# Small matmuls without use behind the groups of the token tail and of the first three expert steps

## What is computed

```python
logits = (X @ gate_w.T).astype(jnp.float32)
scores = jax.nn.sigmoid(logits)
_, idx = jax.lax.top_k(scores + bias[None, :], K)          # K = 4 of E = 32 experts
...
pos = jnp.take_along_axis(jnp.cumsum(onehot, axis=0) - 1, eid[:, None], axis=1)[:, 0]
valid = pos < C
xe = jnp.zeros((E, C, D), x.dtype).at[eid, posc].add(...)
h = jax.nn.silu(jnp.einsum('ecd,edi->eci', xe, W1)) * jnp.einsum('ecd,edi->eci', xe, W3)
ye = jnp.einsum('eci,eid->ecd', h, W2)
...
out = out + jax.nn.silu(X @ sw1.T) * (X @ sw3.T) @ sw2.T   # shared expert
```

## Time and profile before

| | us |
|---|---|
| median of 3 executions | 1815.99 |
| lowest, highest | 1815.87, 1816.35 |
| the profiled execution | 1819.74 |
| its span, first to last instruction | 1817.9 |
| busy: TensorE (PE) | 1654.4 (91%) |
| busy: VectorE (DVE) | 1390.9 (77%) |
| busy: GpSimd (POOL) | 1257.8 (69%) |
| busy: ScalarE (ACT) | 1073.4 (59%) |

### The profile page before, as it was taken

How to read it: one execution, slowest core, us unless ns; L and a number is a source line. 1 busy time by engine, 2 the same in 40 slices (tenths; PEclk the granted TensorE clock), 3 DMA queues, 4 the chain that set the end, 5 groups by cost and what they waited for, 6 DMA issues and landing times.

```text
span 1817.9 us, 31703 instructions
## 1 busy us (share of the span) xinstructions
PE 1654.4 (91%) x8928; PEld 1037.0 (57%) x8928; DVE 1390.9 (77%) x3486; ACT 1073.4 (59%) x2376; POOL 1257.8 (69%) x1105
## 2 busy tenths in 40 slices
PE   6999999999999999999999999997518999999991
PEld 5566666666566666666666566664304555555550
DVE  5679978978997897899789789997505777777771
ACT  5777767767777677677677677764203444444440
POOL 2337777766777777777777777777473787777864
PEclk8999999999999999999999999999759999999996
DMA  7657856666776666677566666666557999999885
GB/s 248 150 130 185 181 151 165 162 158 155 183 177 160 157 169 154 173 175 177 150 150 172 161 172 162 174 155 136 144 168 193 221 234 219 236 211 192 171 137 71
DMA packets 474531, 311.00 MB, mean 171 GB/s; under 512 B 338672, under 2 KB 381426, under 8 KB 474356
## 3 DMA queue, kind: packets, MB, share of 16 engines
q1 hardware_dynamic: 429300, 239.03, 51.2%
q0 software_dynamic: 45056, 69.93, 20.6%
HBM read 135.06 MB, written 110.17 MB: 135 GB/s over the span
## 4 chain that ended last, share of the span: by engine, by line
PE 45%; issue 20%; DVE 14%; ACT 7%; POOL 6%; DMA 3%; another core or an unknown queue 2%; SPq 1%; DVEq 0%; ACTq 0%; POOLq 0%
PE S_ps L481 10%; PE O_ps L496 9%; PE G_ps L523 4%; PE U_ps L523 4%; POOL out L1519 3%; PE GE_ps L1544 3%; PE UE_ps L1544 3%; POOL rows L1507 2%; PE YE_ps L1584 2%; PE PREP_ps L577 2%; DMA out<-ye,idx_far 2%; PE PREP_ps L562 2%; DVE top_s L1240 2%; DVE x_l L1190 1%
## 5 line engine op out<-in xcount | busy, mean ns | idle before, releaser
L897 POOL DMA_INDIRECT slot_table<-tok_line,slot x480 | 510.1, 1063 | 131.8 <-issue 128.0
L906 POOL TENSOR_TENSOR xt_l<-xt,xt_h 128x512 fp32r<-128x512 f32 x128 | 166.2, 1298 | 172.9 <-ACT xt_h L744 172.9
L781 ACT ACTIVATE prob<-S_ps,rs 128x512 f32<-128x512 f32 x128 | 88.0, 688 | 260.5 <-DVE S_ps L1246 157.2
L481 PE MATMUL S_ps<-a_h,xt_h 128*128 128x512 f32 x512 | 222.1, 434 | 0.6 <-DVE m_l L1222 0.6
L496 PE MATMUL O_ps<-m_h,pt_h 128*128 128x512 f16 x512 | 196.2, 383 | 7.7 <-DMA pt_l<-p_l 5.9
L481 PE MATMUL S_ps<-a_h,xt_l 128*128 128x512 f32 x512 | 200.7, 392 | 0.0
L481 PE MATMUL S_ps<-a_l,xt_h 128*128 128x512 f32 x512 | 200.6, 392 | 0.0
L496 PE MATMUL O_ps<-m_l,pt_h 128*128 128x512 f16 x512 | 194.8, 380 | 0.0
L496 PE MATMUL O_ps<-m_h,pt_l 128*128 128x512 f16 x512 | 194.7, 380 | 0.0
L921 POOL TENSOR_TENSOR prob<-prob,rsum 128x512 f32<-128x512 f32 x128 | 135.7, 1060 | 80.6 <-DVE rsum L1277 67.1
L1519 POOL DMA_INDIRECT out<-ye,idx_far x80 | 126.0, 1575 | 50.8 <-issue 31.3
(11 more groups left out here) (242 smaller groups left out, 4800.8 us busy)
## 6 DMA issues: line engine op xcount, KB each, us to landing
xt<-in_xT SPq DMA_DIRECT2D x128, 256.0 KB
xr<-in_x SPq DMA_DIRECT2D x64, 512.0 KB, 3.8
x2aug<-x SPq DMA_DIRECT2D x128, 256.0 KB
out<-xr SPq DMA_DIRECT2D x64, 512.0 KB, 3.1
up_more<-in_w SPq DMA_DIRECT2D x36, 256.0 KB
slot_table<-tok_line,slot POOLq DMA_INDIRECT x512
up_w<-in_w SPq DMA_DIRECT2D x28, 256.0 KB
down_more<-in_w SPq DMA_DIRECT2D x18, 256.0 KB
```

The costliest lines, as they stand in the source:

```text
L481: last = pe.matmul(S_ps[t % 2][:, :], left[:, kc, :], right[:, b % 2, kc, :], start=(m == 0), stop=(m == 3 * KD - 1))
L781: act.activation(prob[:, t % 2, :, :], S_ps[t % 2][:, :].rearrange("p (h j) -> p h j", h=H), ACT.Exp, scale=rs[:, q % 2, 0, t % 2:t % 2 + ...
L897: pool.indirect_dma_start(table, bass.IndirectOffsetOnAxis(ap=slot[:, g % 2, i, q:q + 1], axis=0), tok_line[:, g % 2, i, :], None, bounds_ ...
L906: pool.tensor_tensor(xt_l[:, t % 2, :, :], xt[:, t % 2, :, :], xt_h[:, t % 2, :, :].bitcast(F32), ALU.subtract).then_inc(xt_lo, 1)
```

## The change

A function push(count) issues count matmuls that nobody reads. In the tail they are 128 x 128 in bfloat16, `ones` times `earlier` (two constants), into BOUND_ps, a bank not used any more there; in the experts they multiply two parts of weight set 3 into a bank of the down projection, YE_ps[1], before that bank's real matmuls begin anew. They wait for nothing and raise no semaphore. There are 192 in the tail and 192 in the experts: 16 ahead of the first step, 64 with turn(0,0) to turn(0,3), 80 in the next step, 32 in the one after. One wait is new, for weight set 3, ahead of the expert steps. No other engine's program changes.

```diff
--- before.py
+++ after.py
@@ -654,27 +654,48 @@
                     down_tile(bank, 2 * j).then_inc(g_done, 1)
                     down_tile(other, 2 * j + 1).then_inc(u_done, 1)
 
+                def push(count):
+
+                    for m in range(count):
+                        pe.matmul(BOUND_ps[:, 0:P], ones[:, :], earlier[:, :], start=True, stop=True)
+
                 for n in range(TAIL):
                     step(n)
                 logits(FINAL - 4)
+                push(8)
                 mix(FINAL)
+                push(8)
                 last_up(BUT_ONE, 0)
+                push(8)
                 logits(FINAL - 3)
+                push(24)
                 rank(BUT_ONE)
+                push(16)
                 logits(FINAL - 2)
+                push(8)
                 pe.wait_ge(exp_done, TILES)
                 last_up(BUT_ONE, 1)
+                push(8)
                 logits(FINAL - 1)
+                push(8)
                 logits(FINAL)
+                push(8)
                 pe.wait_ge(prep_lo, B * 8)
                 pe.wait_ge(x1_done, TILES)
                 last_down(BUT_ONE, 0)
+                push(8)
                 last_down(BUT_ONE, 1)
+                push(24)
                 rank(LAST)
+                push(8)
                 last_up(LAST, 0)
+                push(8)
                 last_up(LAST, 1)
+                push(24)
                 last_down(LAST, 0)
+                push(8)
                 last_down(LAST, 1)
+                push(16)
                 pe.wait_ge(exp_done, TILES)
                 pe.wait_ge(x1_done, TILES)
                 pe.wait_ge(scale_step, PAIRB * 5)
@@ -1586,28 +1607,42 @@
                     n += 1
             last.then_inc(y_done, 1)
 
+        def push(count):
+
+            for m in range(count):
+                pe.matmul(YE_ps[1][:, 0:P], up_set(3)[:, 0, 0:P], up_set(3)[:, 0, P:2 * P], start=True, stop=True)
+
         def step(at):
             t, u, d = at(TURN), at(UP), at(DOWN)
             if u is not None:
                 up(u, 0)
+                push(8 if u < 2 else 0)
             if d is not None:
                 down(d, 0)
+                push(8 if d == 0 else 0)
             if t is not None:
                 turn(t, 0)
+                push(16 if t < 3 else 0)
             if d is not None:
                 down(d, 1)
             if t is not None:
                 turn(t, 1)
+                push(16 if t < 2 else 0)
                 turn(t, 2)
+                push(16 if t < 2 else 0)
             if u is not None:
                 up(u, 1)
+                push(8 if u < 1 else 0)
             if t is not None:
                 turn(t, 3)
+                push(16 if t < 2 else 0)
             if d is not None:
                 down(d, 2)
                 down(d, 3)
 
         pe.wait_ge(ident_ready, 1)
+        pe.wait_ge(set_loaded[3], 48)
+        push(16)
         expert_steps(step)
 
     def experts_scalar(act):
```

## The result

The changed kernel takes 1822.79 us (median of 13, 1813.44 to 1830.0), the kernel before 1811.99 in 13 executions beside it (1808.84 to 1818.45). The ratio is 1.0057 with a 95% interval of 1.0038 to 1.0077: slower by 10 us, where 1796 was forecast. It lies inside the range given, on the side that was held the less likely of the two; counted from the base of the prediction, 1815.99, the ratio makes 1826, just over the range's upper end. The profiled execution of the kernel before (1819.74) was its slowest; that of the changed kernel took 1820.24. A single pair of profiles therefore shows places and not the size of the loss, and a second profile of the kernel before stands among the experiments.

What follows compares the result with a forecast made beforehand. Late TensorE signals between token tail and first expert were taken as the bound, with POOL's gathers and scatters next: 1815.99 - 21.1 (earlier first scatter) + 1 (pushes) = 1796 us; range 1783 to 1825.

Steps and rivals of the forecast that it cites:

- the side that was held the less likely of the two: Whole kernel: slower than before, given chance 0.28, against 0.52 for faster and 0.20 for the same.
- the 21 us that POOL's floor allows: First expert step: POOL's first scatter, at 1386.86, cannot start before 1365.76, behind its fifth gather; gain 21.1 us.
- the 34 of TensorE: First expert step: with prompt turn signals up(0,0) could start at about 1332, 34 us earlier.
- The forecast's first step: Expert 0's four turns: pushes following on TensorE bring their late signals out; the tail's wholly or mostly not; chance 0.28.
- The row that spoke against: Token tail: logits(FINAL-4) had 28 large matmuls behind it, over at 1276.55, yet its exponential started only at 1280.44.
- held elsewhere, by POOL's small indirect transfers: Turns and tail: POOL's transfers or the way to the receiver hold signals, pushes do nothing; 1818.6 to 1820.7 us, chance 0.29.
- That price: Each push, in tail and experts: 0.054 us at 2.4 GHz to 0.107 us at 1.2 GHz of TensorE time.
- The sum of what lies on the path, 4.7 us: Pushes on the path if signals gain nothing: 1.7 us in the tail plus 3.0 us in the experts.
- For steps 2 and 3 it was put at 3.0: Second and third expert steps: pushes on the path cost 1.3 and 1.7 us, if the signals gain nothing.
- the wait for weight set 3 cost nothing, as said: Ahead of the expert steps: last load issued at 1298.53, TensorE there at about 1326, so the wait costs nothing.
- The rival on the slower side: Turns and tail: signals come some time after TensorE falls idle, so pushes delay them; 1825 to 1830 us, chance 0.19.

## Why the prediction was wrong

**What bounds the kernel** was read rightly: without the last filings the four signals are in time, and the gain is the 21 us that POOL's floor allows (1815.58 - 1794.62 = 21.0 by the medians, 19.8 by the ratio), not the 34 of TensorE.

**The forecast's first step failed**: that what follows on TensorE brings a signal out. It rested on turn(0,3), 19.6 us late with nothing behind it, against 7.5 us of the others. The 19.6 were counted from the group's own end, the 7.5 from the end of the group behind it; from their own ends turn(0,1) and turn(0,2) are 15.4 and 17.4 us late. Counted from one take to the next, the same rows say 9.86, 9.83 and 11.95 us, some 1.2 to 1.5 us for each of a turn's eight instructions; the last turn takes 2.1 us more, not twice as long. turn(0,3) was issued at 1344.20, while turn(0,2)'s eight still stood ahead of it until 1352.57. The row that spoke against, 28 large matmuls behind logits(FINAL-4) without effect, was right and was weighed too lightly.

**The row that was missed** is POOL's, in the trace of the kernel before:

```profile
1289.90 0.97 POOL L958 DMA_INDIRECT slot_table<-tok_line,slot  x1 [12.46 <-DVE slot L1181]
```

LAST-but-one's filing starts at 1289.90 after 12.46 us of waiting for slots, so POOL's transfers had ended at 1277.44; the bunch of late signals came at 1280.44, 3.0 us behind. In the changed kernel it is 4.0 us (1350.25 to 1354.29), in the run with step 1's pushes 2.5, with the filings ahead 3.2. The rival "held elsewhere, by POOL's small indirect transfers" was therefore the right mechanism. Its price was mis-sized: it let the pushes cost only their TensorE time.

**That price**, 0.054 to 0.107 us for one, is right as long as TensorE is not held up (0.056 measured) and far off where it is: 0.7 to 2.8 us for a matmul with its load. The sum of what lies on the path, 4.7 us, agrees with what the pushes cost with filings left out (3.2 us by the medians, 4.7 by the ratios). For steps 2 and 3 it was put at 3.0, where under 4.5 was found; the wait for weight set 3 cost nothing, as said: in the run with step 1's pushes the first sixteen start at 1314.92, 0.36 us behind VectorE's work on the last bank, as turn(0,0) does in the kernel before.

**The rival on the slower side**, a signal counted from TensorE falling idle, gave the right sign but not the mechanism: behind the last turn of expert 0, after which TensorE falls idle, the signal comes 19.6 us later in the kernel before, 1.9 us later with one matmul per turn (1321.54 to 1323.48) and 0.04 us later without the last filings.

**What stays open**: what it is in POOL's transfers that slows the signing off. Memsets in place of filings don't do it, filings and gathers do. Open, too, is what sets the moment from which TensorE is slow: it is 10.7 us into POOL's block in the changed kernel and 13 us in the changed kernel without the last filings, while twelve gathers in the kernel before without the last filings, whose TensorE has fewer instructions there, did not do it in 16 us, and 23 us of an idle TensorE let two turns through at once. In the steady expert steps, where gathers and scatters alternate and POOL works 40 of 50 us, TensorE works 47.5 of 50. The Trainium skill, "NOTIFIC — the notification-queue block", section "Overflow: three behaviours, one of which stalls the engine", says that the inner stages of the block that writes trace records hold an engine back rather than lose a record. A queue signed off by the instruction would look like that; no run here shows that it is this one. Of the loss, the tail's pushes alone (-3.4 us) and the experts' alone (12.5 us) add up to 9.1, which agrees with the 10.3 of both. But the way to it is not the same: with the experts' pushes alone up(0,0) is late, in the changed kernel it is early and the second step is late. Why step 1's pushes and those of steps 2 and 3 make only half of what they cost together is not settled.

## What to carry to other kernels

Before anything is added to an engine to hurry its signals, measure their lateness from one signal to the next and not from each group's own end: equal steps speak for a queue that is worked off, and then every instruction added makes it longer. Look in that stretch at what the other engines do, and above all for the one whose pause the late signals follow; here taking POOL's back-to-back transfers out gave 20 us, and filler matmuls behind the groups cost 10. Of what was tried within the computation, only the tail's pushes alone and the filings ahead of the gathers were faster than both kernels, by 0.2 to 0.3%.

## What the hardware showed that was not expected

TensorE, with nothing to wait for, issued in steps of 0.70 us or a multiple of it while POOL sent indirect transfers without a pause (0.69, 1.40 and 2.10 us in the rows above), against 0.056 us for a load and a matmul of 128 columns elsewhere, the first ten us of such a block included. Signals were up to 41 us late in that state (1317.28 to 1358.0); where they outlasted POOL's block they came 2.5 to 4.0 us behind its end in the four places dated above. ScalarE's and VectorE's signals to each other were not late in these stretches: in the run with one matmul per turn VectorE follows ScalarE's turns in 0.03 to 0.13 us throughout.
